# Attention loop of a conv, attention and filter kernel on one core: merge and Newton steps with one tensor source, both folds on VectorE, another order of the units

## The reference, cut to what matters

```python
x = x + deformable_conv(_gn(x))                 # bilinear samples of x, 9 per pixel, 4 corners each
t = _to_tokens(x)                               # (8, 1024, 64)
t = t + _L1_attn_ref(_ln_t(t), w_q, w_k, w_v, w_o)
t = t + _L1_ffn_ref(_ln_t(t), ...)              # spectral filter stage
# in _L1_attn_ref, 16 heads of 64, 1024 tokens, causal:
q = _apply_rope(q, cos, sin)
k = _apply_rope(k, cos, sin)
att = einsum('bqhd,bkhd->bhqk', q, k) / sqrt(64)
att = softmax(where(causal, att, -inf))
y = einsum('bhqk,bkhd->bqhd', att, v).reshape(B, S, H * E)
return einsum('bsf,ef->bse', y, w_o)
```

## Time and profile before

| | us |
|---|---|
| median of 3 runs | 3067.74 (3067.49 to 3069.47) |
| the profiled execution | 3066.54 |
| its span | 3064.8 |
| attention loop, 272 to 2356 of the span | 2084 |
| PE busy over the span | 2777.3 (91%) |
| DVE busy | 2275.0 (74%) |
| POOL busy | 1735.3 (57%) |
| ACT busy | 1328.6 (43%) |

### The profile page before, as it was taken

The page is one execution under the profiler, slowest core; times in us unless marked ns, Lnnn a source line. Parts: engine busy times, 40 slices in busy tenths (PEclk is TensorE's granted clock), DMA queues, the critical chain, the costliest instruction groups (busy, mean ns, idle before and its releaser), DMA issues. The chain is left out here.

```text
span 3064.8 us, 60697 instructions
## 1 busy us (share of the span) xinstructions
PE 2777.3 (91%) x18761; PEld 1797.9 (59%) x18761; DVE 2275.0 (74%) x3909; ACT 1328.6 (43%) x1788; POOL 1735.3 (57%) x1832
## 2 busy tenths in 40 slices
PE   3548999999999999999999999999999699999998
PEld 1334555555555555555555555555555588888887
DVE  3547877878778878887878887787788576767676
ACT  1103444444444444444444444444444265656565
POOL 3745766766666677676767667766676581000000
PEclk8658999999999999999999999999999899999999
DMA  5531221222222222122222222224434543434343
GB/s 148 159 93 46 61 60 50 66 56 59 64 56 60 59 60 61 52 65 57 59 61 60 60 55 63 59 55 62 59 60 57 126 158 127 147 119 155 121 145 110
DMA packets 159644, 249.21 MB, mean 81 GB/s; under 512 B 71662, under 2 KB 93502, under 8 KB 159582
## 3 DMA queue, kind: packets, MB, share of 16 engines
q1 hardware_dynamic: 125902, 155.61, 17.8%
q0 software_dynamic: 33680, 92.71, 12.5%
HBM read 230.65 MB, written 17.04 MB: 81 GB/s over the span
## 5 line engine op out<-in xcount | busy, mean ns | idle before, releaser
L1085 ACT ACTIVATE attention_probs<-attention_pss 128x1024 f32<-128x1024 f32 x576 | 589.7, 1024 | 332.0 <-PE attention_pss L922 319.6
L1289 POOL DMA_INDIRECT attention_gat<-table,attention_idx x585 | 556.8, 952 | 200.2 <-issue 126.8
L922 PE MATMUL attention_pss<-attention_kq 64*128 64x512 f32 (+3 forms) x3072 | 652.1, 483 | 0.0
L1024 PE MATMUL attention_psY<-attention_probs,attention_xt 128*64 128x512 f32 (+3 forms) x3120 | 575.3, 497 | 0.2 <-issue 0.2
L1151 DVE TENSOR_REDUCE attention_mx<-attention_pss 128x2 f32<-128x1024 f32 (+3 forms) x520 | 513.6, 1020 | 45.4 <-PE attention_pss L922 45.4
L1246 POOL TENSOR_TENSOR attention_kq<-attention_tA,attention_tB 128x512 f32<-128x512 f32 x260 | 415.1, 1605 | 217.3 <-DVE attention_tB L1161 208.1
L1645 DVE SCALAR_TENSOR_TENSOR spectral_eo<-spectral_psE,kept_sig,spectral_eo 64x512 fp32r<-64x512 f32 x512 | 384.0, 750 | 170.1 <-ACT spectral_eo L1620 163.9
L1538 PE MATMUL spectral_psE<-spectral_tz,spectral_up 128*128 128x512 f32 (+1 forms) x2304 | 461.8, 358 | 6.6 <-DVE spectral_up L1636 6.4
L922 PE MATMUL attention_pss<-attention_rows_m,attention_ones 64*128 64x512 f32 (+2 forms) x1536 | 459.3, 530 | 0.0
L1620 ACT ACTIVATE spectral_eo<-spectral_psE,kept_sig 64x512 fp32r<-64x512 f32 x512 | 349.9, 683 | 244.6 <-PE spectral_psE L1538 239.7
L1538 PEld LDWEIGHTS spectral_psE<-spectral_tz,spectral_up 128*128 128x128 f32 x2304 | 386.2, 189 | 79.0 <-issue 7.2
(11 more groups left out here) (193 smaller groups left out, 3114.7 us busy)
## 6 DMA issues: line engine op xcount, KB each, us to landing
spectral_tz<-phis SPq DMA_DIRECT2D x128, 320.5 KB, 4.6
spectral_tz<-phis SPq DMA_DIRECT2D x128, 320.0 KB, 4.2
attention_xb<-xn SPq DMA_DIRECT2D x132, 256.0 KB, 3.8
attention_gat<-table,attention_idx POOLq DMA_INDIRECT x585
table<-front_pixT SPq DMA_DIRECT2D x32, 288.0 KB
attention_wt<-in_w SPq DMA_DIRECT2D x66, 128.0 KB, 3.6
attention_xt<-xt SPq DMA_DIRECT2D x18, 128.0 KB, 2.1
attention_xs<-in_x SPq DMA_DIRECT2D x65, 32.0 KB
```

The costliest lines, as they stand in the source:

```text
L922: ins = pe.matmul(out(n), left(rows), right(rows), **flags)
L1024: ins = pe.matmul(psY[C * n:C * n + C, q:q + w], xt[:, kt, :], probs[:, u, n, at:at + w], start=(u < 2), stop=(u == NU - 1), skip_group_ch ...
L1085: act.activation(probs[:, u[1], :, :].rearrange("p n q -> p (n q)"), pss[:, slot, :], ACT.Exp, scale=float(E) ** -0.5).then_inc(s_act, 1)
L1289: pool.indirect_dma_start(gat[:, n, :, :].rearrange("p q c -> p (q c)"), None, d.table.rearrange("r q c -> r (q c)"), bass.IndirectOffsetO ...
```

## The change

Four edits, all in the attention stage:

1. `merge` reads one tensor: the two maxima of query tiles 4 to 7 are written side by side into a new buffer `mx_half`, and one reduction takes the larger; before, a tensor_tensor combined `mx` and `mx_far`.
2. The Newton steps of `norm` become tensor_scalar instructions: the second factor is read as a scalar per partition, not as a second tensor. Their number stays three for each of the three rounds.
3. `fold 0` leaves GpSimd's order and stands in SEQUENCE, so VectorE does it, right ahead of `fold 1`.
4. `SEQUENCE`, `POOL_ORDER` and `AHEAD` are written in another order.

```diff
-SEQUENCE = [("rope", 0), ("rope", 1), ("weigh", 0), ("upper", 0), ("rope", 2), ("upper", 1), ("value", 2, 1),
+SEQUENCE = [("value", 3, 1), ("rope", 0), ("rope", 1), ("S", 0), ("S", 1), ("rope", 2), ("upper", 0),
...
-        mx_far = sb("mx_far", [P, 2, NT // 2])
+        mx_half = sb("mx_half", [P, 2, NT // 2, 2])
...
-                            ins = dve.tensor_reduce(mx_far[:, :, i - 4] if k0 else mx[:, :, i], scores, AX.X, ALU.max)
+                            ins = dve.tensor_reduce(mx[:, :, i] if i < 4 else mx_half[:, :, i - 4, k0 // 4], scores, AX.X, ALU.max)
...
-                    dve.tensor_tensor(mx[:, :, NT // 2:NT], mx[:, :, NT // 2:NT], mx_far[:, :, :], ALU.max).then_inc(s_mx, 1)
+                    dve.tensor_reduce(mx[:, :, NT // 2:NT], mx_half[:, :, :, :], AX.X, ALU.max).then_inc(s_mx, 1)
...
-                        step(dve.scalar_tensor_tensor(out=fix[:, :], in0=rstd[:, :], scalar=-0.5, in1=rstd[:, :],
-                                                      op0=ALU.mult, op1=ALU.mult))
+                        step(dve.tensor_scalar(fix[:, :], rstd[:, :], rstd[:, 0:1], -0.5, ALU.mult, ALU.mult))
                         step(dve.tensor_scalar(fix[:, :], fix[:, :], var[:, 0:1], 1.5, ALU.mult, ALU.add))
-                        step(dve.tensor_tensor(rstd[:, :], rstd[:, :], fix[:, :], ALU.mult))
+                        step(dve.tensor_scalar(rstd[:, :], rstd[:, :], fix[:, 0:1], None, ALU.mult))
```

More of the change, by code:

```diff
@@ L652, in uppers_of @@
     return max(K_AT[k0 // 4], Q_AT[i // 4])
-SEQUENCE = [("rope", 0), ("rope", 1), ("weigh", 0), ("upper", 0), ("rope", 2), ("upper", 1), ("value", 2, 1),
-            ("weigh", 1), ("value", 3, 1), ("value", 4, 1), ("S", 0), ("rope", 3), ("upper", 2), ("S", 1),
-            ("max", "a"), ("value", 5, 1), ("weigh", 2), ("value", 6, 1), ("max", "d"), ("max", "g"), ("upper", 3),
-            ("max", "h"), ("leave",), ("value", 7, 1), ("value", 8, 1), ("S", 2), ("fold", 1), ("S", 3),
[3 rows of a table removed]
-            ("row",)]
-POOL_ORDER = [("add", 0), ("add", 1), ("add", 2), ("mask", 0), ("add", 3), ("fold", 0), ("gather", 0),
-              ("gather", 1), ("mask", 2), ("token", 0), ("mask", 4), ("gather", 2), ("mask", 7), ("mask", 8),
-              ("token", 1)]
+SEQUENCE = [("value", 3, 1), ("rope", 0), ("rope", 1), ("S", 0), ("S", 1), ("rope", 2), ("upper", 0),
+            ("weigh", 0), ("value", 4, 1), ("upper", 1), ("weigh", 1), ("value", 5, 1), ("value", 6, 1), ("upper", 2),
+            ("value", 7, 1), ("max", "a"), ("max", "b"), ("rope", 3), ("weigh", 2), ("S", 2), ("S", 3),
+            ("leave",), ("max", "c"), ("max", "f"), ("value", 8, 1), ("fold", 0), ("S", 4), ("fold", 1),
+            ("S", 5), ("max", "d"), ("upper", 3), ("S", 6), ("max", "h"), ("value", 0, 0), ("max", "g"),
+            ("dT",), ("out", 0), ("max", "j"), ("max", "k"), ("dR",), ("norm",), ("S", 7),
+            ("S", 8), ("max", "i"), ("max", "e"), ("value", 1, 0), ("merge",), ("value", 2, 0), ("dX",),
+            ("out", 1), ("row",)]
+POOL_ORDER = [("add", 0), ("add", 1), ("mask", 0), ("add", 2), ("add", 3), ("gather", 0), ("mask", 2),
+              ("mask", 4), ("gather", 1), ("token", 0), ("gather", 2), ("mask", 7), ("mask", 8), ("token", 1)]
 AHEAD = [("rope", 0), ("rope", 1), ("upper", 0), ("upper", 1), ("rope", 2), ("rope", 3), ("upper", 2),
-         ("upper", 3), ("max", "a"), ("max", "d"), ("max", "c"), ("max", "b"), ("max", "g"), ("max", "h"),
-         ("max", "e"), ("max", "f"), ("max", "k"), ("max", "i"), ("max", "j"), ("merge",), ("row",)]
+         ("upper", 3), ("max", "a"), ("max", "b"), ("max", "c"), ("max", "d"), ("max", "f"), ("max", "h"),
+         ("max", "g"), ("max", "e"), ("max", "j"), ("max", "k"), ("max", "i"), ("merge",), ("row",)]
 BY_ACT = ("S", "row", "dT", "dR")
```

## The result

| | us |
|---|---|
| before, median of 4 runs | 3068.37 (3067.49 to 3069.47) |
| after, median of 4 runs | 3025.06 (3023.63 to 3026.95) |
| ratio | 0.9859 (95% interval 0.9842 to 0.9876) |
| the profiled execution after, its span | 3026.95, 3025.2 |

A forecast was written before the change was run, and what follows sets the result against it. PE was taken to bound the attention loop, waiting at row for VectorE's merge. Bodies falling from 65.70 to 64.0 us save 54 us, the clock 27: 3067.7 - 81 = 2987 us, range 2952 to 3024.

The forecast's parts named there:

- Merge 0.17, from 1.54: VectorE's merge ahead of row: as a one-source reduction, no longer held by GpSimd's token additions, 0.17 us instead of 1.54.
- Norm 3.88 to 3.73: Norm on VectorE: Newton products lose 0.45 us of waiting, pointer scalars cost 0.3 back, so 3.88 becomes 3.73 us.
- rival 2: Late row DMAs behind gathers, or norm's scaling held by GpSimd: 0.5 us more per pair, 3019 us; 0.22 with another rival.
- Fold 0 at 1.36, cost 0: Fold 0 on VectorE between max f and max d: takes 1.36 us, costs PE nothing under two S units.
- PE's own sum 30.9 and small waits 0.25: PE per pair: matmuls 30.9 us, from 31.20 with two fewer switches, plus an estimated 0.25 of small waits.
- S 0 sees its row at 3.35, waits 0.4: S 0 behind row: 2.93 us of PE work, row DMAs seen at 3.35, so a new wait of 0.4 us.
- Merge against row: 0.4: From out 0 to row: VectorE's chain 9.0 us against PE's 8.6, so row still waits 0.4 us.
- The last ten pairs like the others: End of the attention loop: no separate term; all 32 bodies were taken to save 1.7 us each, 54 us.
- No fall of the clock, 27 us: Attention loop: PE's shorter waits avoid all 16 falls to 1.2 GHz, at 1.69 us each, saving 27 us.

The follow-up runs named there:

- e2: The kernel before, in its own order, with only the merge as a reduction: 2953.2 us, ratio 0.9621.
- e3: The kernel after with the old merge, a tensor_tensor of two tensors: 3021.8 us, ratio 0.9839.
- e8: The kernel after with two Newton rounds instead of three: 3008.9 us, ratio 0.9793.
- e13: The kernel after with padding tiles' indices filled from real tiles and one Newton round instead of three: 2990.1 us, ratio 0.9748.
- e14: The kernel after with padding tiles' indices filled and max e moved from behind norm to behind max f: 3031.6 us, ratio 0.9877.
- e18: The kernel after with padding tiles' indices filled, one Newton round, and the last gather group ahead of token 0: 2951.1 us, ratio 0.9622.
- e1: The kernel after with the padding tiles' cleared gather indices filled with real tiles' indices: 3005.4 us, ratio 0.9789.
- e12: The kernel after with padding tiles' indices filled and max j ahead of dT and out 0: 3025.8 us, ratio 0.9859.
- e16: The kernel after with padding tiles' indices filled and the last gather group ahead of token 0: 3004.0 us, ratio 0.9794.
- e17: The kernel after with padding tiles' indices filled, max e behind max f, and the last gather group ahead of token 0: 2999.5 us, ratio 0.9779.

## Why the prediction was wrong

- *Merge 0.17, from 1.54.* Right: 169 to 171 ns. The Trainium skill, page "SBUF — State Buffer", section "Who interferes with whom", says that on this chip a tensor_reduce never contends with GpSimd: the traces agree, here beside the issue of gathers and in e2 beside a mask (169 to 173 ns). The prediction laid the old 1.54 us to the token addition alone; two masks held the merge first. And it did not ask whether the order alone would free the tensor_tensor; it does (e3, 168 ns).
- *Norm 3.88 to 3.73.* 3.76 (1215.90 to 1219.66), products at 0.21: right. In the old order Newton gave 0.11 per pair. Norm's scaling was not held here (0.31 in all 61), though token 0 runs beside it: that half of rival 2 acts only in e8, e13 and e14, where norm ends earlier against token 0 (up to 0.54 us at the scaling and 0.57 at the copy, e13).
- *Fold 0 at 1.36, cost 0.* 1.35, and by the ratio 0 in this order: right. In the old order it costs 0.1 to 0.17.
- *PE's own sum 30.9 and small waits 0.25.* 31.15 together, and e18's 31.52 less its S 0 wait of 0.4 is 31.1: right, as far as one kernel without the other wait can tell. Matmuls and small waits were not told apart.
- *S 0 sees its row at 3.35, waits 0.4.* 3.34, right, for the first 54 pairs. Rival 2's mechanism, gathers that move bytes when the row DMAs run, does not act there: the gathers' bytes end 0.15 us ahead of the row's second burst (e1), and e8 loses 0.15 as soon as the row comes earlier.
- *Merge against row: 0.4.* The failed step of the body. I counted from out 0 and found VectorE 0.4 behind at row. e12 showed that the start is dR (6.45 us from its end to row, as before, with VectorE idle ahead of norm): ScalarE's read, norm, i, and there it meets out 1 first, through the slot, which I had not looked at; then e, merge and row. Two stops instead of one, and 0.79 us where I had 0.4. That is the 0.32 to 0.36 per pair, 18 us.
- *The last ten pairs like the others.* The failed step of the end. Rival 2 named late row DMAs at 0.5 us per pair for all pairs; it was 1.8 us for ten. The trace of before shows the crowded DMA engines in that stretch (0.16 MB of gathers took 30.3% of their time from 2184 to 2189 us); I read DMA only near 1217 us. 20 us by e1. Rival 2's total, 3019, is the one nearest to 3025, and by luck: what it counts over 64 pairs fell in ten, and larger.
- *No fall of the clock, 27 us.* One fall instead of 16, and none in e1: right. But e2 shows the same without the new order, so these 27 us and the 88 of merge belong to edit 1, or to the order, and not to both.

## What to carry to other kernels

When a change holds several edits, price each alone on the kernel before: here three lines gave 115 us, and the order written beside them took back some 80. Follow a slot as well as a semaphore: the unit three ahead of the one that waits says who must have read. A short lead between a small DMA and its reader holds only while the DMA engines are quiet at that moment, so look for what the same engines carry at the end of the loop, where padding work runs. And when a chain on VectorE gets shorter, look again at what GpSimd does beside its end.

## What the runs showed of the hardware

- Gathers whose indices all name one table row held the DMA engines for 63.3% of 5 us with 0.39 MB; with spread indices it was 20.6% with 0.34 MB.
- A tensor_tensor of VectorE with two SBUF sources takes 166 to 169 ns beside GpSimd's issue of gathers (e3), and 1.54 us beside two of its masks and a token addition.
- A 4 KB DMA whose turn falls among gathers' bytes is seen later by its reader: S 0 starts 3.3 us behind row where they keep apart (e16, e17, e18), and 3.5 to 4.0 where they meet (e8, e13, and e14 in the body).
- A tensor_scalar and a copy within SBUF are held by a token addition too. Norm's scaling takes 0.86 us in e13 instead of 0.31. In e8 norm's last copy falls beside token 0, and takes up to 612 ns instead of 195:

```profile
L1207 DVE COPY attention_xt_new<-attention_xn x62: 199/587/612, 313.9 to 2289.8; 128x63 f32<-128x63 f32 x62
```
